# Four graph layers on one core: root products ahead of the upper sums, and column marks made by ScalarE

## The chip, the cores and the metric

The kernel runs on one core of a Trainium2 chip. Its metric is the device time of one execution in microseconds; the time before is 4219.57 us, the median of three runs (4215.5 to 4219.84).

## The reference

A graph of 100000 nodes with 16 features and 50000 edges passes through four layers. Each layer normalises the nodes (`h = relu(layernorm(x))`), makes a message for each edge from the features at one end of it, sums the messages over the edges that share the other end, and adds to x. Cut to what matters:

```python
edge_index = jnp.stack([src, dst])
h = relu(_layernorm(x)); x = x + clip(h + segment_sum(h[src] * ew * w, dst) + slw * h, 0, 1)
h = relu(_layernorm(x)); x = x + segment_sum(sum_k basis[e, k] * (h[dst] @ W[k]), src)
h = relu(_layernorm(x))
# third layer, once from src to dst and once in reverse, 8 outputs each:
#   g = relu(layernorm(h) * ln_g + ln_b)
#   out = segment_sum(einsum(g[src], (edge_attr @ We + be)), dst) + g @ Wr + bias
x = x + concatenate([out_n, out_r])
h = relu(_layernorm(x))
# fourth layer: m = silu(einsum(h[dst], edge_attr, W_msg)) @ W_lin, agg = segment_sum(m, src)
x = x + h + silu(einsum(h, agg, W_upd)) @ W_upd_lin
```

`g @ Wr + bias` are the third layer's root products: a product for every node, whatever its edges.

## The kernel before, in words

The nodes lie as 128 partitions by 784 nodes by 16 features in SBUF (`x`, `h`). The edges are sorted twice in a first part (by dst and by src), one record per edge, into two tables in HBM; blocks of 14 nodes per partition (`BC`) take their edges in tiles of 128 edges. A sorted edge list has 448 tiles, handled 8 at a time, so that each layer has 56 groups, in 14 rounds of 4 (`RING`).

In a group of the edge stage (`edges(l)` and, for PE and POOL, the loops of the same stage):

- SP loads the records of the group (`rec`), as soon as the group four before it has been spread out (`e["spread"]`) and its marks are made (`e["lo"]`).
- POOL gathers the rows of the table of h by eight indirect DMAs (L478), one for each tile.
- PE transposes the rows (L636), ScalarE copies or scales them to `featT` (L847, L850), PE multiplies them with the layer's weights: products 0 and 1 at L608, 2 and 3 at L584 (`late_product`). The products 2 and 3 share PSUM with the sums.
- VectorE (DVE) multiplies the products with the edge's attributes (L1244, L1257, L1272), reduces them to one message an edge (L1249, L1265, L1277) in `raw`, and spreads the message over the 14 columns (nodes) of its block with the column marks `at_hi` (L1197, `spread_out`): a mark is 1 in the column of the edge's node and 0 elsewhere. DVE makes the marks itself, in `columns` (L1192): `is_equal` of the numbers 0 to 13 and the record's field.
- ScalarE makes the partition marks `at_lo`, 128 wide, from eight Abs (L830) and a Relu (L834): relu(1 - |number - node|) is 1 where both are equal.
- PE sums over the edges by a matmul with those marks, tile by tile (L563), one group behind: in the second and third layers four tiles in `upper_sums`, four in `lower_sums`, the lower ones behind the products' use by DVE. Each fp32 matmul shows as two passes in the trace, so four tiles are `x8`.
- DVE adds the sums tile by tile to a running sum (L1219, `run`), also one group behind, and SP writes it to HBM (`scan`). In these two layers `run` starts only when all eight sums are there.

In the third layer root products are put into the gaps. A group does 2, 2, 2 or 1 blocks of 128 columns of nodes (`BLOCKS`): ScalarE copies a part of h to `rootH` (L838), PE transposes it (L615), ScalarE makes `rootT` (L855), PE multiplies it with `Wroot` into `psR` (`root_products`, L625), and DVE adds that and the bias to x at the group's end (`root`, L1301 and L1303). `psR` shares its PSUM bank with `raw`, so DVE's reduction L1265 waits for the root products of its group (`root_s["sums"]`). The root products wait for `rootT` (`rowsS`) and for DVE's add of the group before (`added`).

Each engine works through its instructions in the order in which the program writes them; the waits are semaphores set by hand. Of the code these lines set the order on PE:

```python
for m in range(2, 4):
    late_product(g, m)
if not first:
    upper_sums(g)
if l == 2:
    root_products(i, k, first)
if not first:
    lower_sums(g)
```

In the first and fourth layers PE's group ends with the sums and matmuls without use (`spin`, L543) between them; in the second they stand behind the lower sums; the third has none. Between the edge stages lie node stages (`nodes(l)`), which read the sums from HBM, add them to x, normalise and store the table. `W4` is a weight table for the last part (the update of the fourth layer), made by DVE (L1341) from a product of PE.

## Time and profile before

| | |
|---|---|
| median of three runs | 4219.57 us |
| profiled execution | 4218.45 us |
| its span | 4216.7 us |
| PE, DVE, ScalarE (ACT), POOL busy | 2432.8, 2864.7, 1201.1, 2737.6 us |
| first sorting and its placing by POOL | to about 562 us |
| edges of the first layer | 562 to 1126 us |
| placing of the second table by POOL | 1126 to 1628 us |
| edges of the second layer | 1628 to 2263 us |
| nodes, then edges of the third layer | 2263 to 2409, then to 3097 us |
| nodes, then edges of the fourth layer | 3097 to 3193, then to 3765 us |
| update of the fourth layer | 3765 to 4217 us |

The span runs from the first to the last instruction of the profiled execution. A stage's own limit is read from its own stretch, since busy shares over the whole span mix four kinds of stage. A group's time is the distance between two starts of the same instruction in neighbouring groups. In the rows, `xN` merges N neighbours of one line, and the bracket at the end tells how long the engine stood idle and what released it.

### The profile page before, as it was taken

The page shows a single profiled execution, that of the slowest core. Times are in us where ns is not written, and L with a number is a line of the kernel's source. Part 1 is how long each engine was busy: PE and PEld are TensorE (multiplying, and loading weights), DVE is VectorE, ACT ScalarE, POOL GpSimd, SP SyncE. Part 2 cuts the span into 40 slices and gives each one's busy share as a digit, 9 for nine tenths or more (in the row PEclk, how much of TensorE's full clock was granted, in tenths as well). Part 3 has the DMA queues.
Part 4 walks back from the last instruction along what each step waited for, and adds up shares of the span by engine and source line. Part 5 has one row for each costly group of instructions (what it writes and reads, how often), then busy time and mean ns, then how long its engine had stood idle before and what let it go on. Part 6 is the DMA issues. An engine that isn't in the chain of part 4 may idle for free.

```text
span 4216.7 us, 32712 instructions
## 1 busy us (share of the span) xinstructions
PE 2432.8 (58%) x9418; PEld 1746.0 (41%) x9418; DVE 2864.7 (68%) x4332; ACT 1201.1 (28%) x3002; POOL 2737.6 (65%) x2799
## 2 busy tenths in 40 slices
PE   1200038788600003888883077777725988979998
PEld 1100037777500002656562055555513777753333
DVE  8893035666580003999998877777776887868887
ACT  1000023333430002444443244444413343421111
POOL 3777777777777777776660176666505777746776
PEclk7555579999855556888886577777767999985556
DMA  6011023333630001333344222222532333351010
GB/s 181 9 26 52 8 51 111 103 111 103 104 114 12 5 5 28 99 90 98 94 94 98 83 77 91 91 92 92 82 126 91 102 108 100 109 91 30 26 35 27
DMA packets 200536, 321.45 MB, mean 76 GB/s; under 512 B 83898, under 2 KB 166698, under 8 KB 199971
## 3 DMA queue, kind: packets, MB, share of 16 engines
q1 hardware_dynamic: 112848, 265.61, 17.8%
q0 software_dynamic: 82368, 21.64, 8.1%
q10 hardware_dynamic: 5140, 32.09, 2.0%
q8 instruction: 76, 1.25, 0.1%
q14 instruction: 104, 0.85, 0.1%
HBM read 66.90 MB, written 252.21 MB: 76 GB/s over the span
## 4 chain that ended last, share of the span: by engine, by line
POOL 39%; DVE 24%; issue 19%; PE 14%; ACT 2%; DMA 1%; SPq 1%; POOLq 0%; DVEq 0%
POOL rows L478 21%; POOL edges_by_dst L462 9%; POOL edges_by_src L462 9%; DVE work L1219 8%; PE psX L720 6%; PE psK L563 5%; DVE natD L1244 3%; DVE psX L1249 3%; PE psX L625 2%; DVE natS L1354 1%; DVE psX L1265 1%; DVE h L1105 1%; ACT work L830 1%; PE psK L700 1%; DVE psX L1102 1%
## 5 line engine op out<-in xcount | busy, mean ns | idle before, releaser
L478 POOL DMA_INDIRECT rows<-table,rec x1792 | 1692.2, 944 | 996.5 <-issue 522.8
L563 PE MATMUL psK<-work 128*128 128x224 f32 x3584 | 974.2, 429 | 518.3 <-DVE work L1197 292.5
L563 PEld LDWEIGHTS psK<-work 128*128 128x128 f32 x3584 | 816.0, 236 | 704.4 <-issue 646.8
L1219 DVE SCALAR_TENSOR_TENSOR work<-work,keep,psK 128x224 f32<-128x224 f32 x1792 | 800.9, 447 | 109.6 <-PE psK L563 52.1
L830 ACT ACTIVATE work<-iota,rec 128x128 f32<-128x128 f32 x1792 | 546.0, 391 | 575.4 <-PE psK L563 358.1
L543 PE MATMUL psX<-keep,ident 128*128 128x256 f32 x2648 | 636.3, 388 | 0.0
L543 PEld LDWEIGHTS psX<-keep,ident 128*128 128x128 f32 x2648 | 520.9, 197 | 63.0 <-issue 1.5
L462 POOL DMA_INDIRECT edges_by_dst<-natD,pos x391 | 374.6, 958 | 184.2 <-issue 127.0
L462 POOL DMA_INDIRECT edges_by_src<-natS,pos x391 | 374.4, 958 | 127.3 <-issue 127.3
L1197 DVE TENSOR_TENSOR work<-at_hi,psX 128x1792 f32<-128x1792 f32 x224 | 452.2, 2019 | 6.2 <-ACT psX L872 0.4
L636 PE MATMUL psX<-ident,rows 128*128 128x128 f32 x168 | 49.7, 296 | 657.0 <-DMA rows<-table,rec 657.0
L509 POOL TENSOR_TENSOR work<-natS 128x512 f32<-128x512 f32 x196 | 243.4, 1257 | 156.2 <-DVE natS L1354 156.2
L850 ACT ACTIVATE natD<-psX 128x128 f32<-128x128 f32 x112 | 31.0, 277 | 1049.2 <-PE psX L636 1049.2
L720 PE MATMUL psX<-natD,work 32*128 32x512 f32 x784 | 303.9, 1036 | 18.8 <-DVE natS L1354 18.1
L636 PEld LDWEIGHTS psX<-ident,rows 128*128 128x128 f32 x168 | 23.8, 142 | 682.4 <-issue 497.5
L1228 DVE TENSOR_TENSOR psX<-rows,rec 128x128 f32<-128x128 f32 x56 | 16.9, 301 | 425.3 <-DMA rows<-table,rec 425.3
L1354 DVE TENSOR_TENSOR natS<-psX,h 128x1024 f32<-128x1024 f32 x196 | 238.5, 1217 | 73.1 <-PE psX L720 73.0
L1237 DVE TENSOR_TENSOR natD<-hats 128x128 f32<-128x128 f32 x56 | 15.9, 284 | 382.1 <-ACT hats L821 382.1
L834 ACT ACTIVATE work<-work,one 128x1024 f32<-128x1024 f32 x224 | 257.2, 1148 | 7.3
L584 PE MATMUL psK<-natD 32*128 32x512 f32 (+1 forms) x448 | 210.1, 601 | 67.0 <-DVE work L1219 66.7
L608 PE MATMUL psX<-natD 32*128 32x512 f32 (+2 forms) x672 | 173.6, 594 | 91.3 <-ACT natD L847 50.2
L1265 DVE TENSOR_REDUCE psX<-natD 128x64 f32<-128x576 f32 x112 | 79.5, 756 | 130.8 <-PE psX L625 130.8
(149 smaller groups left out, 2478.4 us busy)
## 6 DMA issues: line engine op xcount, KB each, us to landing
scan<-work SPq DMA_DIRECT2D x224, 896.0 KB
rows<-table,rec POOLq DMA_INDIRECT x1792
table<-h ACTq DMA_DIRECT2D x28, 896.0 KB, 3.6
work<-scan SPq DMA_DIRECT2D x168, 112.0 KB, 2.0
rec<-edges_by_dst SPq DMA_DIRECT2D x112, 84.0 KB, 1.9
natD<-scan SPq DMA_DIRECT2D x56, 112.0 KB, 2.0
edges_by_dst<-natD,pos POOLq DMA_INDIRECT x391
edges_by_src<-natS,pos POOLq DMA_INDIRECT x391
```

The source lines that it names most:

```text
L462: pool.indirect_dma_start(out=rec_by[s].ap(), out_offset=bass.IndirectOffsetOnAxis(ap=pos[s][0:n, u:u + 1], axis=0), in_=nat[0:n, u * F:(u ...
L478: pool.indirect_dma_start(out=rows[k][:, u * D:(u + 1) * D], out_offset=None, in_=table.ap(), in_offset=bass.IndirectOffsetOnAxis(ap=rec[k ...
L509: nc.gpsimd.tensor_tensor(hf, w[:, :, :, 0:8], w[:, :, :, 8:16], ALU.add).then_inc(up["half"], 1)
L543: nc.tensor.matmul(psT[:, 256:512], ident[:, :], keep[0][:, 0:256], start=True, stop=True)
L563: nc.tensor.matmul(psK[:, o:o + BW], at_lo[par][:, t * P:(t + 1) * P], spread[par][:, t * BW:(t + 1) * BW], start=True, stop=True)\
L584: nc.tensor.matmul(psK[:, (m - 2) * 512:(m - 2) * 512 + w.shape[1]], featT[row:row + high, s * P:(s + 1) * P], w[row:row + high, :], start ...
L720: k = nc.tensor.matmul(psQ[q % 2][:, j * 512:(j + 1) * 512], rt[two, b * P:(b + 1) * P], W4[two, m * 512:(m + 1) * 512], start=True, stop= ...
L830: a = S.activation(at_lo[par][:, t * P:(t + 1) * P], iota1[:, :], ACT.Abs, bias=field(l, k, LO[ORDER[l]])[:, t, :])
L834: S.activation(at_lo[par], at_lo[par], ACT.Relu, scale=-1.0, bias=one[:, :]).then_inc(e["lo"], 1)
L1197: V.tensor_tensor(spread[par].rearrange("p (u c f) -> p u c f", c=BC, f=D), v3(at_hi[par][:, :], BC)[:, :, :, None].to_broadcast([P, G, BC ...
L1219: V.scalar_tensor_tensor(acc[par][:, t * BW:(t + 1) * BW], was, keep[s][:, bass.ds(q * G + t, 1)], psK[:, o:o + BW], ALU.mult, ALU.add).th ...
L1354: V.tensor_tensor(products(q)[0], psQ[q % 2].rearrange("p (u k i) -> p u k i", k=D, i=D), v3(h[:, bass.ds(c * CW + 64 * q, 64)])[:, :, Non ...
```

## The change

Three things change.

1. In PE's order of the third layer `root_products` stands ahead of `upper_sums`, behind the late products.
2. The column marks `at_hi` are made by ScalarE (`column_of`: eight Abs of 128x14 and one Relu of 128x112), ahead of the partition marks, in every group of every layer. The wait for the sums of two groups before (`summed`) now stands ahead of both. `columns` is gone from DVE, and L1197 waits for a new semaphore `cols`. The record's field has the other sign, so that Abs can take it as bias.
3. DVE makes `W4` behind the node stage of the third layer, no longer at the end of the second layer's edges.

```diff
                         for m in range(2, 4):
                             late_product(g, m)
+                        if l == 2:
+                            root_products(i, k, first)
                         if not first:
                             upper_sums(g)
-                        if l == 2:
-                            root_products(i, k, first)
                         if not first:
                             lower_sums(g)
...
-                def partition_of(i, k, started):
+                def column_of(i, k):
 
                     par = k % 2
-                    if started:
-                        act.wait_ge(e["summed"], i * (RING * G) + (k - 1) * G)
+                    for t in range(G):
+                        a = S.activation(at_hi[par][:, t * BC:(t + 1) * BC], iota14[:, :], ACT.Abs,
+                                         bias=field(l, k, HI[ORDER[l]])[:, t, :])
+                    a.then_inc(e["colsraw"], 1)
+                    act.wait_ge(e["colsraw"], i * RING + (k + 1))
+                    S.activation(at_hi[par][:, :], at_hi[par][:, :], ACT.Relu, scale=-1.0, bias=one[:, :])\
+                        .then_inc(e["cols"], 1)
+
+                def partition_of(i, k):
...
-                    partition_of(i, k, started)
+                    if started:
+
+                        act.wait_ge(e["summed"], i * (RING * G) + (k - 1) * G)
+                    column_of(i, k)
+                    partition_of(i, k)
...
-                own.did(V.scalar_tensor_tensor(fields[:, :, HI[s]], ki[5][:, 0:NAT], -float(BC), ki[3][:, 0:NAT],
-                                               ALU.mult, ALU.add))
+                own.did(V.scalar_tensor_tensor(fields[:, :, HI[s]], ki[5][:, 0:NAT], float(BC), ki[3][:, 0:NAT],
+                                               ALU.mult, ALU.subtract))
...
-                def columns(i, k):
-
-                    dve.wait_ge(rec_in[k], i * 16 + (PAST_REC[l] + 16))
-                    own.did(V.tensor_tensor(v3(at_hi[k % 2][:, :], BC), iota14[:, None, :].to_broadcast([P, G, BC]),
-                                            field(l, k, HI[s]).to_broadcast([P, G, BC]), ALU.is_equal))
-
-                def spread_out(k):
+                def spread_out(i, k):
                     par = k % 2
+                    dve.wait_ge(e["cols"], i * RING + (k + 1))
...
-                edges(l)
-                if l == 1:
+                if l == 2:
                     dve.wait_ge(w4_psum, 1)
...
                     k.then_inc(w4_ready, 1)
+                edges(l)
```

The third layer on PE, one group with two blocks of nodes, before: the rows that wait name the semaphores (`r_` those of the root products, `e2_` those of the third layer's edges).

```order
L563 MATMUL psK<-work 128x224 [waits e2_run,e2_lo,e2_spread]
L563 MATMUL psK<-work 128x224 x3
L625 MATMUL psX<-natD 128x128 [waits r_added,r_rowsS]
L625 MATMUL psX<-natD 128x128 x3
L563 MATMUL psK<-work 128x224 [waits e2_used]
L563 MATMUL psK<-work 128x224
L563 MATMUL psK<-work 128x224 [waits e2_used]
L563 MATMUL psK<-work 128x224
L615 MATMUL psX<-ident,natD 128x128 [waits r_rows,gath2]
```

And now:

```order
L625 MATMUL psX<-natD 128x128 [waits r_added,r_rowsS]
L625 MATMUL psX<-natD 128x128 x3
L563 MATMUL psK<-work 128x224 [waits e2_run,e2_lo,e2_spread]
L563 MATMUL psK<-work 128x224 x3
L563 MATMUL psK<-work 128x224 [waits e2_used]
L563 MATMUL psK<-work 128x224
L563 MATMUL psK<-work 128x224 [waits e2_used]
L563 MATMUL psK<-work 128x224
L615 MATMUL psX<-ident,natD 128x128 [waits r_rows,gath2]
```

The four matmuls of the root products, which wait for DVE's add of the group before, have come ahead of the four upper sums; the eight sums now lie behind one another, up to the next group's transposes.

The third layer on ScalarE, one group, now (L856 and L864 are the lines L847 and L855 of before, L847 here is L838, L839 and L843 are L830 and L834):

```order
L856 ACTIVATE natD<-psX,shift,gain 128x128 [waits e2_bandT]
L856 ACTIVATE natD<-psX,shift,gain 128x128
L864 ACTIVATE natD<-psX,shift,gain 128x256 x2
L847 ACTIVATE natD<-h 128x256
L828 ACTIVATE at_hi<-iota,rec 128x14 [waits e2_summed,rec1]
L828 ACTIVATE at_hi<-iota,rec 128x14 x7
L832 ACTIVATE at_hi<-at_hi,one 128x112 [waits e2_colsraw]
L839 ACTIVATE work<-iota,rec 128x128 x8
L843 ACTIVATE work<-work,one 128x1024 [waits e2_abs]
```

The three rows of `at_hi` are new and stand between the copy of h and the partition marks; all else is in its old order.

## Rows read from the trace of the kernel before

**Rows 1.** Busy time in four stretches, the edges of the four layers; the columns are named.
```profile
core 0: us, PE busy (x) PEld busy (x) DVE busy (x) ACT busy (x) POOL busy (x), PEclk, DMA share, GB/s
562.00:1126.00 564.00, 442.15 (x1944) 391.69 (x1944) 333.66 (x644) 201.15 (x505) 423.74 (x449) 0.92 0.38 101
1628.00:2263.00 635.00, 541.37 (x1849) 376.77 (x1850) 594.86 (x889) 275.47 (x840) 422.76 (x448) 0.81 0.33 90
2409.00:3097.00 688.00, 489.26 (x1890) 377.67 (x1890) 519.32 (x1007) 302.80 (x783) 423.40 (x448) 0.78 0.32 86
3193.00:3765.00 572.00, 497.15 (x2219) 395.76 (x2219) 443.35 (x707) 223.24 (x606) 422.70 (x448) 0.96 0.37 98
```

**Rows 2.** Waits of DVE in the third layer: in total, times, longest.
```profile
DVE psX L1265 <- PE psX L625: 125.2, 53, 3.1
```

**Rows 3.** Timeline of one third-layer group: start us, us, engine, line, instruction.
```profile
2624.58 3.33 PE L563 MATMUL psK<-work 128*128 128x224 f32 x8 [1.28 <-DVE work L1219]
...
2627.70 1.10 PE L625 MATMUL psX<-natD 128*128 128x128 f32 x8
...
2628.64 1.68 PE L563 MATMUL psK<-work 128*128 128x224 f32 x8
...
2628.91 1.42 DVE L1265 TENSOR_REDUCE psX<-natD 128x64 f32<-128x576 f32 x2 [2.04 <-PE psX L625]
...
2630.36 2.02 DVE L1197 TENSOR_TENSOR work<-at_hi,psX 128x1792 f32<-128x1792 f32 x1
...
2632.30 3.82 DVE L1219 SCALAR_TENSOR_TENSOR work<-work,keep,psK 128x224 f32<-128x224 f32 x8
...
2632.48 2.44 ACT L830 ACTIVATE work<-iota,rec 128x128 f32<-128x128 f32 x8
...
2636.04 0.41 DVE L1301 TENSOR_TENSOR x<-x,psX 128x256 f32<-128x256 f32 x1
```

**Rows 4.** The same timeline, PE: starts of the sums, root products and transposes.
```profile
2600.98 3.19 PE L563 MATMUL psK<-work 128*128 128x224 f32 x8 [1.28 <-DVE work L1219]
...
2612.08 3.33 PE L563 MATMUL psK<-work 128*128 128x224 f32 x8 [1.27 <-ACT work L834]
...
2618.74 0.38 PE L615 MATMUL psX<-ident,natD 128*128 128x128 f32 x2
...
2630.16 0.38 PE L615 MATMUL psX<-ident,natD 128*128 128x128 f32 x2
...
2636.27 3.33 PE L563 MATMUL psK<-work 128*128 128x224 f32 x8 [1.03 <-DVE work L1219]
...
2639.39 1.91 PE L625 MATMUL psX<-natD 128*128 128x128 f32 x8
...
2642.79 0.27 PE L615 MATMUL psX<-ident,natD 128*128 128x128 f32 x1
...
2648.77 1.46 PE L563 MATMUL psK<-work 128*128 128x224 f32 x3 [1.27 <-DVE work L1219]
```

**Rows 5.** Timeline of a second-layer group, DVE and ScalarE.
```profile
1804.89 0.91 ACT L817 ACTIVATE hats<-rec,hatb 128x16 f32<-128x16 f32 x4
...
1806.09 2.43 ACT L830 ACTIVATE work<-iota,rec 128x128 f32<-128x128 f32 x8
...
1808.69 0.28 DVE L1237 TENSOR_TENSOR natD<-hats 128x128 f32<-128x128 f32 x1
...
1808.90 0.27 DVE L1192 TENSOR_TENSOR at_hi<-iota,rec 128x112 f32<-128x112 f32 x1
...
1809.19 1.29 DVE L1244 TENSOR_TENSOR natD<-psX,natD 128x512 f32<-128x512 f32 x2
...
1814.04 2.02 DVE L1197 TENSOR_TENSOR work<-at_hi,psX 128x1792 f32<-128x1792 f32 x1
```

**Rows 6.** The same stretch, POOL: one of eight gathers of a group.
```profile
1809.27 0.94 POOL L478 DMA_INDIRECT rows<-table,rec  x1 [0.30 <-issue]
```

**Rows 7.** Timeline, DVE: the table W4, and the first product of layer three.
```profile
2266.54 3.91 DVE L1341 TENSOR_SCALAR natD<-psX,rowmask 128x256 f32<-128x256 f32 x8
...
2423.68 0.82 DVE L1257 TENSOR_TENSOR natD<-psX,rec 128x288 f32<-128x288 f32 x2 [17.95 <-PE psX L608]
```

More of the change, by code:

```diff
@@ L238, in build_gnn @@
         names = ("taken", "bandT", "bandS", "prod", "used", "preact", "silu", "hats", "hatsraw",
-                 "abs", "lo", "spread", "summed", "run")
+                 "abs", "lo", "colsraw", "cols", "spread", "summed", "run")
         lacks = [("bandT", "bandS", "prod", "used", "preact", "silu", "hats", "hatsraw"),
@@ L822, in hat_factors @@
                         .then_inc(e["hats"], 1)
-                def partition_of(i, k, started):
+                def column_of(i, k):
                     par = k % 2
-                    if started:
-                        act.wait_ge(e["summed"], i * (RING * G) + (k - 1) * G)
+                    for t in range(G):
[6 more added lines that the diff above has]
+                def partition_of(i, k):
+                    par = k % 2
                     for t in range(G):
@@ L1183, in nodes_twice @@
                 own.close()
-            STEPS = [2, 3, 3, 1]
+            STEPS = [1, 2, 2, 0]
             def edges(l):
                 s, e = ORDER[l], ed[l]
-                def columns(i, k):
-                    dve.wait_ge(rec_in[k], i * 16 + (PAST_REC[l] + 16))
-                    own.did(V.tensor_tensor(v3(at_hi[k % 2][:, :], BC), iota14[:, None, :].to_broadcast([P, G, BC]),
-                                            field(l, k, HI[s]).to_broadcast([P, G, BC]), ALU.is_equal))
-                def spread_out(k):
+                def spread_out(i, k):
                     par = k % 2
+                    dve.wait_ge(e["cols"], i * RING + (k + 1))
                     V.tensor_tensor(spread[par].rearrange("p (u c f) -> p u c f", c=BC, f=D),
@@ L1229, in messages @@
                                         field(l, k, D_EW).to_broadcast([P, G, D]), ALU.mult).then_inc(e["taken"], 1)
-                        columns(i, k)
                         dve.wait_ge(e["taken"], g + 1)
@@ L1239, in messages @@
                                                 hv[:, :, 1, None, :].to_broadcast([P, G, 4, 4]), ALU.mult))
-                        columns(i, k)
                         own.settle()
@@ L1251, in messages @@
                     elif l == 2:
-                        columns(i, k)
                         for m in range(4):
@@ L1268, in messages @@
                     else:
-                        columns(i, k)
                         for m in range(2):
@@ L1288, in group @@
                     own.settle()
-                    spread_out(k)
+                    spread_out(i, k)
                     if l != 3 and not first:
```

## The prediction

> **What bounds the kernel now.** I read the busy times by stage first [rows 1]. In the first layer's edges POOL, with its eight gathers a group, sets the pace: 564 us over 56 groups are 10.1 us a group, and eight gathers of 0.94 us with 0.30 us between them are about 10.0 [rows 6]. The fourth layer is alike (572 us with filling and draining). The second layer is another case: VectorE (DVE) is busy 594.86 of 635 us, a group takes about 11.0 us, more than POOL needs. The third layer, 688 us, is the slowest: neither DVE (519) nor POOL (423) nor PE (489) fills it, so the engines wait for one another. What that wait is, the waits of DVE say: 53 times, 125.2 us in all, its reduction L1265 stands until PE's root products L625 are done, 2.36 us a time [rows 2]. The timeline of one group shows why [rows 3]: PE first does the four upper sums (L563, 3.12 us until the next instruction), which nobody wants yet, and only then the root products, for which DVE stands 2.04 us. The upper sums come in a stretch of low clock: eight passes take 3.33 us there, 1.68 us in the lower half. Four groups take 47.79 us, 11.95 each [rows 4]. That is the number to beat.
>
> **Part 1, the order on PE in the third layer.** Nothing is added, four or eight passes of L625 move ahead of eight passes of L563. Two limits remain for DVE.
>
> First, its own work. From group to group 11.69 us went by (PE 2624.58 to 2636.27), of which DVE waited 2.04: 9.65 us of work, and 0.19 us less without the columns (part 2), 9.46.
>
> Second, a wait that takes the place of the old one. DVE's running sums L1219 want all eight sums of the group, and these now stand behind the root products; the root products in turn want DVE's add L1301 of the group before (semaphore r_added), which is behind its running sums. So the loop is: running sums 3.74 us until the add (2632.30 to 2636.04), add 0.41, release of PE 0.15 (2636.12 to 2636.27), PE's block of 24 passes, release of DVE 0.1 (an estimate, from the 0.15 of PE). Today the block, from the first upper sum to the next transposes L615, takes 6.66, 5.58 and 6.52 us [rows 3, 4], 6.25 on average, with eight root passes. With four root passes (every fourth group) it is shorter by half of L625's time, between 0.47 and 0.95, say 0.7: 5.55. The loop is 4.40 plus the block: 10.65 and 9.95, on average 10.5 us, if PE's clock stays as it is. It was granted 0.78 of full speed in this stage and 0.81 in the second layer, where PE is busy 541 of 635 us; the third layer now keeps PE busy 489 of 688, 8.7 us a group, and at about 10.3 us a group that share is the second layer's 0.85. So I take 0.81 and a block shorter by 4%: 6.02 and 5.35, groups of 10.42 and 9.75, on average **10.25 us**. Bounds: above, 10.5 with the clock of today; below, POOL's 10.0. Saving (11.95 - 10.25) x 54 groups = **92 us**; bounds 78 and 105. I count 54 of 56, since the first group has no sums and the last none after it.
>
> **Part 2, the columns.** DVE loses 224 instructions of 0.27 us (L1192). In the second layer, where DVE is the bound, L1244 starts 0.29 us after L1192; without it, it starts when L1237 is done, at 1808.97 plus the usual 0.03, so 0.19 us earlier [rows 5]: 56 x 0.19 = **10.6 us**. In the third layer this lies inside the loop's wait in most groups; in the first and fourth POOL sets the time: nothing.
> ScalarE gets nine instructions for each. The nearest row: four Abs of 16 columns and one Relu of 64 take 1.20 us (1804.89 to 1806.09), 0.20 per Abs and 0.40 for the Relu, so eight and one are 2.05 us. The upper bound is the pace of the 128-column Abs, 2.43 us for eight, plus 0.4: 2.8. Who waits? The new wait is DVE's: the spreading L1197 now waits for `cols` too. In the second layer the columns would be ready at 1808.14 and the spreading starts at 1814.04: 5.9 us of room. In the third, ScalarE is ready for them 0.2 us after DVE's running sums start (2632.48 against 2632.30); but in the new order PE's block ends, and the transposes start, only 0.1 us ahead of those, not 2.14, so ScalarE comes 2.2 us after. The next spreading is 9.46 - 1.94 = 7.5 us after the start of the running sums (1.94 is 2630.36 to 2632.30), so the room is 7.5 - 2.2 - 2.05 = 3.2 us. Behind the columns stand ScalarE's own Abs of the marks `at_lo`, wanted by PE one group later, and the Silu of the fourth layer, which DVE wants only after a whole turn of running sums. The load fits: in the first layer ScalarE is busy 3.6 us a group, in the third 5.4, plus 2.05. SP's refill of `rec` waits for `lo` as well, and `lo` still comes before the spreading ends or close to it, three groups ahead of its use. Term: 0.
>
> **Part 3, the table W4.** Eight instructions, 3.91 us together (L1341), go from the end of the second layer to behind the third layer's node stage. There they run while DVE waits 17.95 us for the first gather [rows 7]; where they were, DVE waited for a load anyway. PE is held until they are done, but has nothing to do earlier. Term: 0; if that cover were gone, 3.9 us.
>
> **Sum.** 92 + 10.6 = 102.6 us off the profiled execution's 4218.45, 4115.9; the median of the runs is 1.1 higher: **4117 us**.
>
> **Rivals.**
> A, PE at full clock through the third layer. The block is then about 4.3 us (0.94 us for the root products as between 2627.70 and 2628.64, and 1.68 twice), the loop 8.7, and POOL's 10.0 is the bound: (11.95 - 10.0) x 54 = 105, in all 4219.6 - 115.9 = 4104 us. For it: the clock was 0.92 and 0.96 in the layers that keep PE busy with filler. Against: the second layer is as full as this will be and has 0.81. The Trainium skill, "TensorE: Matmul & The Clock Gate", Part 1, says that the throttled clock is the default and activity releases it; by that rule alone a denser PE gives this time. The first and fourth layers agree with it, the second only in part.
> B, the block stays as long as today or gets longer, because root products and upper sums now both fall in the slow stretch: 10.5 to 10.9 us a group, 78 to 57 us saved there, 4131 to 4152 us.
> C, ScalarE's columns come late, and all of it ends slower. It decides from 3.2 us of room: nine instructions above 5.3 us make DVE wait, above 7.3 us the gain is gone. At 8 us (0.9 each) the third layer's group is 10.25 + 2.7 = 12.95, 54 us more than today, less 10.6: 4263 us. Against: a 16-column activation takes 0.31 us at most in [rows 5], a third of that. The Trainium skill, "ScalarE: Activation LUTs", Rules for kernel authors, sends relu, max, add and mul to VectorE; by it one DVE instruction of 0.27 us becomes 2.05 us of ScalarE for nothing. On this trace that holds for work and not for time, as DVE is the engine waited for.
> D, PE at low clock throughout the third layer: a block of 3.12 + 1.7 + 3.12 = 7.9 us, 12.3 and 11.5 a group, 12.1 on average: 8 us lost, 10.6 won, 4217 us, no change.
>
> **Chances.** Forecast 0.67, A 0.13, B 0.15, C 0.02, D 0.03. About 0.2% (8 us) is what a measurement of this kernel can tell from no change. The forecast, A and B are faster: 0.95; D is the same, 0.03; C slower, 0.02. The range takes in A and the better half of B, since both bounds of the block lie in it: 4098 to 4142 us.
>
> **What would show it.** Third layer: about 10.25 us from group to group, stage near 595 us, L1265's wait on L625 under 0.3 us, a new wait of DVE L1219 for PE L563 of about 0.8 us on average, uneven from group to group, clock near 0.81. Second layer: 10.8 us a group, DVE still without a gap. First and fourth: same length. ScalarE about 2 us a group busier, no wait of L1197's successor for it. Wrong if the third layer's group is above 10.6 or exactly POOL's 10.0, or if DVE waits for ScalarE's Relu.

## The result and the profile after

The changed kernel takes **4111.34 us**, median of four runs (4110.35 to 4116.54), against 4219.36 for the kernel before beside it. The ratio is 0.9748, 95% interval 0.9732 to 0.9765: 108 us or 2.5% faster, 6 us below the forecast of 4117 and inside its range. The profiled span is 4108.9 us, before it was 4216.7.

Where the time went is told by the length of each layer's edges, from its first gather's start to the end of its last running sum:

| layer | before | after | difference | forecast |
|---|---|---|---|---|
| first | 581.3 | 580.3 | -1.0 | 0 |
| second | 636.0 | 626.0 | -10.0 | -10.6 |
| third | 687.5 | 592.1 | -95.4 | -92 |
| fourth | 590.5 | 585.1 | -5.4 | 0 |

These differences come to 111.9 us, the span's to 107.8; the first sorting, the placing of the second table and the update of the fourth layer are 1.0, 1.1 and 1.8 us longer in the trace after. From the end of the second layer's edges to the third's first gather there are 142.8 us before and 142.7 after, so the table W4 costs nothing in its new place.

The page after: the engines, and the chain of work that ended last. Line numbers of VectorE (DVE) are shifted: running sums L1219 is L1227 now, the spreading L1197 is L1205, the reduction L1265 is L1270, the product L1257 is L1262, the add L1301 is L1305.

```profile
PE 2346.3 (57%) x9418; PEld 1697.5 (41%) x9418; DVE 2832.2 (69%) x4108; ACT 1634.5 (40%) x5018; POOL 2738.8 (67%) x2799
...
POOL 45%; DVE 21%; issue 20%; PE 11%; DMA 2%; SPq 1%; ACT 0%; POOLq 0%; DVEq 0%
```

POOL is in 45% of the chain (39% before) and PE in 11% (14%). ScalarE's 1634.5 us are 433 more than the 1201.1 before, for 2016 more instructions. That is 1.93 us for each of 224 groups; the forecast said about 2.

Busy time in the edges of the second and third layers after, the view of [rows 1]: length, busy time (and instructions) of PE, its weight loads, DVE, ScalarE and POOL, granted clock, DMA share, GB/s.

```profile
1628.00:2250.00 622.00, 528.93 (x1832) 371.24 (x1832) 582.52 (x828) 385.40 (x1344) 423.57 (x449) 0.81 0.34 91
2395.00:2995.00 600.00, 413.29 (x1890) 332.86 (x1890) 518.25 (x961) 413.12 (x1288) 423.75 (x448) 0.82 0.39 101
```

The third layer's PE is busy 413 us for the same 1890 matmuls as in [rows 1], where it was 489, with a granted clock of 0.82 instead of 0.78. DVE is busy 518 us of 600, before it was 519 of 688: what is gone is waiting.

The waits of the third layer after (2450 to 2980 us), against [rows 2] (2450 to 3080 us): in total, times, longest.

```profile
PE psX L615 <- DMA rows<-table,rec: 55.0, 31, 4.9
...
PE psX L625 <- DVE x L1305: 45.0, 34, 1.6
DVE work L1227 <- PE psK L563: 16.6, 16, 1.5
DVE psX L1270 <- PE psX L625: 13.7, 20, 1.3
```

The 125.2 us for which DVE stood at the reduction are 13.7; over the whole layer 130.8 us are 16.2. The wait that takes its place, the running sums for the upper sums, is 16.6 us in 16 groups. PE now waits, for DVE's add (45.0 us) and for the gathered rows (55.0 us).

POOL's gathers of the third layer, before and then after: shortest, median and longest in ns, then the start of the first and of the last.

```profile
L478 POOL DMA_INDIRECT rows<-table,rec x448: 938/944/1185, 2409.4 to 3051.4; - x150
```
```profile
L478 POOL DMA_INDIRECT rows<-table,rec x448: 940/944/1192, 2400.5 to 2959.6; - x150
```

Before, they were spread over 642.0 us, and POOL stood 95.6 us in 42 waits for the records (`rec`), which SP loads only when an earlier group has been spread out. After, they take 559.1 us, 10.0 us a group from the first to the last, as in the first and fourth layers (558.8 and 558.0 us); the waits for records are gone. Of the layer's 95.4 us, 82.9 lie in this stretch and the rest behind the last gather (45.4 us before, 33.1 after).

Two groups of the third layer after, the view of [rows 3, 4], first with a low clock in PE's block and then without:

```profile
2869.03 2.04 PE L625 MATMUL psX<-natD 128*128 128x128 f32 x8 [1.60 <-DVE x L1305]
...
2870.87 5.26 PE L563 MATMUL psK<-work 128*128 128x224 f32 x16
...
2871.18 1.42 DVE L1270 TENSOR_REDUCE psX<-natD 128x64 f32<-128x576 f32 x2 [0.38 <-PE psX L625]
...
2875.96 0.38 PE L615 MATMUL psX<-ident,natD 128*128 128x128 f32 x2
...
2876.16 3.83 DVE L1227 SCALAR_TENSOR_TENSOR work<-work,keep,psK 128x224 f32<-128x224 f32 x8 [1.51 <-PE psK L563]
...
2878.29 1.68 ACT L828 ACTIVATE at_hi<-iota,rec 128x14 f32<-128x14 f32 x8
...
2880.00 0.39 ACT L832 ACTIVATE at_hi<-at_hi,one 128x112 f32<-128x112 f32 x1
...
2880.30 2.43 ACT L839 ACTIVATE work<-iota,rec 128x128 f32<-128x128 f32 x8
...
2880.47 1.13 PE L625 MATMUL psX<-natD 128*128 128x128 f32 x8 [1.60 <-DVE x L1305]
...
2881.44 3.19 PE L563 MATMUL psK<-work 128*128 128x224 f32 x16
...
2883.73 2.02 DVE L1205 TENSOR_TENSOR work<-at_hi,psX 128x1792 f32<-128x1792 f32 x1
...
2884.47 0.27 PE L615 MATMUL psX<-ident,natD 128*128 128x128 f32 x1
...
2885.67 3.82 DVE L1227 SCALAR_TENSOR_TENSOR work<-work,keep,psK 128x224 f32<-128x224 f32 x8
```

In the first, root products and sums take from 2869.03 to the transposes at 2875.96, 6.93 us, and DVE's running sums stand 1.51 us. In the second the same 24 passes take 4.00 us (2880.47 to 2884.47), and DVE has no wait. ScalarE's columns take from 2878.29 to 2880.30, where its next work starts: 2.01 us. The spreading that needs them starts at 2883.73, 3.3 us after the Relu's end. POOL's gathers come every 1.25 us.

The same two blocks in the view of [rows 1]; the clock granted to PE is the figure after the last bracket, 0.57 and 1.00 of full speed.

```profile
2869.03:2875.96 6.93, 6.93 (x24) 6.49 (x25) 5.21 (x8) 2.64 (x7) 5.10 (x7) 0.57 0.45 146
2880.47:2884.47 4.00, 4.00 (x25) 3.95 (x26) 3.93 (x8) 3.40 (x9) 2.99 (x4) 1.00 0.66 236
```

### The profile page after: what moved, and what is told of

The parts are those of the page before. It is cut to its first block, busy times and chain, and to the rows that moved or that the text cites. A ratio compares the mean times of both kernels' runs of the same rounds, so it can differ in the third digit from the quotient of the medians.

```text
span 4108.9 us, 34672 instructions
## 1 busy us (share of the span) xinstructions
PE 2346.3 (57%) x9418; PEld 1697.5 (41%) x9418; DVE 2832.2 (69%) x4108; ACT 1634.5 (40%) x5018; POOL 2738.8 (67%) x2799
## 3 DMA queue, kind: packets, MB, share of 16 engines
q8 instruction: 76, 1.25, 0.1%
## 4 chain that ended last, share of the span: by engine, by line
POOL 45%; DVE 21%; issue 20%; PE 11%; DMA 2%; SPq 1%; ACT 0%; POOLq 0%; DVEq 0%
POOL rows L478 27%; POOL edges_by_dst L462 9%; POOL edges_by_src L462 9%; DVE work L1227 7%; PE psX L720 6%; DVE natD L1250 3%; DVE psX L1255 3%; PE psK L563 2%; DVE natS L1358 1%; DMA rows<-table,rec 1%; PE psK L700 1%; DVE h L1118 1%; DVE psX L1115 1%; PE psK L691 1%; PE psX L625 0%
## 5 line engine op out<-in xcount | busy, mean ns | idle before, releaser
L563 PE MATMUL psK<-work 128*128 128x224 f32 x3584 | 904.6, 409 | 450.0 <-DVE work L1205 292.4
L563 PEld LDWEIGHTS psK<-work 128*128 128x128 f32 x3584 | 783.6, 225 | 602.6 <-issue 552.5
L1227 DVE SCALAR_TENSOR_TENSOR work<-work,keep,psK 128x224 f32<-128x224 f32 x1792 | 801.2, 447 | 120.7 <-PE psK L563 62.4
L828 ACT ACTIVATE at_hi<-iota,rec 128x14 f32<-128x14 f32 x1792 | 375.2, 296 | 463.2 <-PE psK L563 245.7
L839 ACT ACTIVATE work<-iota,rec 128x128 f32<-128x128 f32 x1792 | 544.3, 386 | 0.0
L1205 DVE TENSOR_TENSOR work<-at_hi,psX 128x1792 f32<-128x1792 f32 x224 | 452.3, 2019 | 8.2 <-ACT psX L885 2.4
L1244 DVE TENSOR_TENSOR natD<-hats 128x128 f32<-128x128 f32 x56 | 15.9, 285 | 383.0 <-ACT hats L821 383.0
L843 ACT ACTIVATE work<-work,one 128x1024 f32<-128x1024 f32 x224 | 257.3, 1149 | 7.2
L753 ACT ACTIVATE work<-h 128x1792 f32<-128x1792 f32 x28 | 47.5, 1697 | 374.7 <-DVE h L1118 374.7
```

The costliest lines, as they stand in the source:

```text
L563: nc.tensor.matmul(psK[:, o:o + BW], at_lo[par][:, t * P:(t + 1) * P], spread[par][:, t * BW:(t + 1) * BW], start=True, stop=True)\
L828: a = S.activation(at_hi[par][:, t * BC:(t + 1) * BC], iota14[:, :], ACT.Abs, bias=field(l, k, HI[ORDER[l]])[:, t, :])
L839: a = S.activation(at_lo[par][:, t * P:(t + 1) * P], iota1[:, :], ACT.Abs, bias=field(l, k, LO[ORDER[l]])[:, t, :])
L843: S.activation(at_lo[par], at_lo[par], ACT.Relu, scale=-1.0, bias=one[:, :]).then_inc(e["lo"], 1)
L1205: V.tensor_tensor(spread[par].rearrange("p (u c f) -> p u c f", c=BC, f=D), v3(at_hi[par][:, :], BC)[:, :, :, None].to_broadcast([P, G, BC ...
L1227: V.scalar_tensor_tensor(acc[par][:, t * BW:(t + 1) * BW], was, keep[s][:, bass.ds(q * G + t, 1)], psK[:, o:o + BW], ALU.mult, ALU.add).th ...
```

## The experiments

The runs fall in two sets. In one, four kernels run on chip 5, the kernel before took 4216.3 us, close to the 4219.36 above. In the other, eight kernels on the chips 9, 4 and 14, it took 5059 to 5079 us itself, and the profile differs in kind. They are told apart, the first set first; ratios are against the kernel before in the same set.

**e5_cols3: more work for ScalarE.** Does the room that part 2 of the prediction gives ScalarE exist, and how large is it?

```diff
+for t in range(2 * G):
+    S.activation(scrap[:, t * BC:(t + 1) * BC], iota14[:, :], ACT.Abs,
+                 bias=field(l, k, HI[ORDER[l]])[:, t % G, :])
 (ahead of the eight Abs of the columns, in every group)
```

> The changed kernel with 24 Abs for the columns in every group, sixteen of them into a scratch tile: 3.3 us more work of ScalarE a group. My theory: the third layer's ScalarE then has 7.4 + 3.3 = 10.7 us of work a group and becomes the bound, and the columns use up the room of 3.2 us: group 10.7 to 11.0 us, 25 to 45 us more than the changed kernel; second layer 0 (7.1 + 3.3 of 10.8 us, room 5.9). Rival: columns so early that all is hidden, 0; or all of it on the path, 3.3 us a group, 180 us.

4140.34 us, ratio 0.9817 (0.9802 to 0.9832), 29 us above the changed kernel. The layers take 580.2, 628.5, 619.1 and 588.3 us. The third layer of e5_cols3 from 2642 on, and DVE's wait of that layer:

```profile
2643.02 3.25 ACT L829 ACTIVATE scrap<-iota,rec 128x14 f32<-128x14 f32 x16
...
2647.88 0.39 ACT L836 ACTIVATE at_hi<-at_hi,one 128x112 f32<-128x112 f32 x1
...
2648.37 2.02 DVE L1209 TENSOR_TENSOR work<-at_hi,psX 128x1792 f32<-128x1792 f32 x1 [0.58 <-ACT at_hi L836]
...
2653.47 3.25 ACT L829 ACTIVATE scrap<-iota,rec 128x14 f32<-128x14 f32 x16
```
```profile
DVE work L1209 <- ACT at_hi L836: 40.4, 48, 2.5
```

The expectation held: the group takes 10.67 us and the kernel 29 us more. ScalarE's turn is 10.45 us (2643.02 to 2653.47) with no gap, and the spreading waits for its Relu 48 times, 0.84 us each. So an added 3.25 us more than uses up the room in the third layer. In the second layer, where the prediction gave 5.9 us, nothing is seen: its 628.5 us are those of e6_spin too, which has no extra Abs. Nor in the first. Rival C's mechanism exists, and the change stays below it. The prediction let it begin at 5.3 us of columns; here they take 5.25 (2643.02 to 2648.27) and DVE waits already, as ScalarE's whole turn has become the group. Where between 2.01 and 5.25 us the wait begins, no run of this set shows.

**e6_spin: fillers ahead of the root products.** Rival A said that a PE at full clock would leave POOL's gathers as the bound, at 10.0 us a group and 4104 us.

```diff
     late_product(...)
 if l == 2:
+    pe.wait_ge(root_s["rowsS"], g + 1)
+    spin(2)
+if l == 2:
     root_products(i, k, first)
```

> The changed kernel with two filler matmuls (four passes) between the late products and the root products of the third layer, where PE waits 1.6 us for DVE's add. They keep PE's clock up. My theory (blocks of 7.1 us at low clock are what is left above POOL's pace, blocks at full clock take 4.16): third layer's group 10.21 to 10.0, granted clock above 0.9, 8 to 14 us less than the changed kernel, 4098 to 4104. Rival (the fillers delay the root products, and the pace is POOL's anyway): 0 or a few us more.

4106.6 us (4101.69 to 4110.08), ratio 0.9737 (0.9724 to 0.975). The interval overlaps the changed kernel's, so the 5 us between the medians are not told from nothing. Expected were 8 to 14 us and a clock above 0.9, and neither came. The third layer takes 588.6 us, 10.11 us a group against 10.21, with 2114 matmuls:

```profile
2403.00:2992.00 589.00, 434.77 (x2114) 340.75 (x2114) 510.67 (x954) 412.93 (x1287) 424.18 (x448) 0.89 0.37 100
```
```profile
DVE psX L1273 <- PE psX L625: 28.4, 21, 2.6
```
```profile
PE psX L615 <- DMA rows<-table,rec: 67.2, 43, 4.6
```

The clock is 0.89; the changed kernel has 0.83 in the same stretch. The running sums have no wait left but one at the layer's end (the reduction has 28.4 us in 21 groups), and in four neighbouring groups the sixteen sums took 3.19 us each. Yet the gathers take 559.5 us from first to last, for 559.1 in the changed kernel; only the time behind the last of them is shorter, 29.2 for 33.1 us. A quicker PE had nothing more to give, as POOL was not being held back.

**e8_seven: the same with seven gathers of eight.** Is POOL the bound that is reached?

```diff
+GATHERS = [8, 8, 7, 8]
-for u in range(G):
+for u in range(GATHERS[l]):
 (the waits for the gathers count 16 * GATHERS[l])
```

> The kernel with fillers and seven gathers a group in the third layer (the eighth tile of each group keeps an older group's rows, so the third layer's messages of one tile in eight are left wrong). Theory (with PE at full clock, POOL's eight gathers at 10.0 us a group are the bound): group down to DVE's own 9.46 us, 25 to 30 us less than the kernel with fillers. Rival (DVE or PE is the bound already): 0, apart from the 1.25 us of a first group's gathering.

The kernel leaves out one gather of eight in the third layer, so that one tile in eight takes the rows of an older group.

4074.17 us, ratio 0.966 (0.9645 to 0.9675): 32.4 us below e6_spin, somewhat more than the 25 to 30 expected. The third layer takes 556.0 us, a group 9.54, and past its start PE no longer waits for gathered rows:

```profile
2403.00:2960.00 557.00, 451.85 (x2114) 343.77 (x2114) 509.33 (x952) 412.97 (x1287) 370.41 (x392) 0.92 0.36 106
```
```profile
DVE psX L1274 <- PE psX L626: 5.7, 9, 1.3
```

DVE stands there 5.7 us in 480 us of the layer, and POOL now waits for records (41.6 us), so 9.54 is DVE's own work; the prediction had 9.46 for it. The gathers thus hold e6_spin back by 0.57 us a group. In the changed kernel both limits are near: the gathers at 10.0 us, unheld from first to last, and the loop over PE and DVE at about 10.26.

**e7_old_order_spin: columns on ScalarE, order as before, fillers.** It was to raise PE's clock without the new order, and so to part the two.

```diff
     late_product(...)
+if l == 2:
+    pe.wait_ge(root_s["rowsS"], g + 1)
+    spin(2)
 if not first:
     upper_sums(g)
+if l == 2:
+    root_products(i, k, first)
 (against the changed kernel; W4 stands at its old place too)
```

> The columns alone (old order on PE) with the same two filler matmuls ahead of the upper sums. It asks whether the order or the clock was worth the gain. At full clock the upper sums take 1.5 us and the root products 0.94, so the root products would be ready 0.5 to 1.0 us after DVE asks for them, not 2.4. My theory: group 10.2 to 10.9 us, 55 to 95 us less than the kernel before, that is, the low clock was most of the price of the old order. Rival (the order itself is the price): group over 11.4 us, under 35 us less.

4203.59 us, ratio 0.997 (0.9958 to 0.9982). The layers take 581.2, 626.1, 690.0 and 584.4 us. Third layer of e7_old_order_spin: its window, DVE's wait, and one group of the timeline.

```profile
2401.00:3091.00 690.00, 553.30 (x2114) 419.31 (x2114) 509.10 (x952) 412.87 (x1287) 423.56 (x448) 0.78 0.31 86
```
```profile
DVE psX L1273 <- PE psX L625: 122.1, 47, 3.8
```
```profile
2605.66 2.07 PE L543 MATMUL psX<-keep,ident 128*128 128x256 f32 x4
2607.53 3.19 PE L563 MATMUL psK<-work 128*128 128x224 f32 x8
...
2611.68 1.68 PE L563 MATMUL psK<-work 128*128 128x224 f32 x8
...
2611.95 1.42 DVE L1273 TENSOR_REDUCE psX<-natD 128x64 f32<-128x576 f32 x2 [3.68 <-PE psX L625]
```

The clock did not rise, 0.78 as before: the two filler matmuls (four passes) fell in the slow stretch themselves and took 2.07 us, where in 31 of 56 groups of e6_spin they took 1.13. So this kernel doesn't part clock and order, and its expectation (55 to 95 us less) was missed. It does something else: it is the columns and fillers without the order. The second layer has its 10 us less (626.1), the fourth its 6 less (584.4), and the third is no shorter (690.0 against 687.5), with a wait of 122.1 us at the reduction.

Against e6_spin it differs in nothing but PE's order and the place of W4, which costs nothing (142.7 us between the stages in both). So the order, with columns and fillers on both sides, is worth 101.4 us in the third layer (690.0 against 588.6) and 97.0 us of the kernel (4203.59 against 4106.6).

**The other set.** Here the same kernel before takes 5059 to 5079 us; no trace of it is kept. The nearest is e3_w4, which is the kernel before but for the place of W4 (5084.43 us, below). The kernel before of the first set and then e3_w4, a row each on DVE's running sums and on PE's filler matmuls: count, busy time, mean ns, then the idle time ahead of them and what ended it.

```profile
L1219 DVE SCALAR_TENSOR_TENSOR work<-work,keep,psK 128x224 f32<-128x224 f32 x1792 | 800.9, 447 | 109.6 <-PE psK L563 52.1
...
L543 PE MATMUL psX<-keep,ident 128*128 128x256 f32 x2648 | 636.3, 388 | 0.0
```
```profile
L1219 DVE SCALAR_TENSOR_TENSOR work<-work,keep,psK 128x224 f32<-128x224 f32 x1792 | 801.7, 447 | 1138.0 <-remote 893.2
...
L543 PE MATMUL psX<-keep,ident 128*128 128x256 f32 x2648 | 729.1, 412 | 264.7 <-issue 261.3
```

A running sum takes 447 ns in both. But ahead of them stand 1138.0 us of idle time for 109.6, of which 893.2 were ended by something that the trace only calls remote (it ran on one core), and ahead of PE's fillers 261.3 us ended by nothing that the profile shows ("issue"), where there was none. The first layer, 581 us before, takes 1126 us in e3_w4 and 1310 in e11_order_again. PE in the first layer of e11_order_again:

```profile
1205.82 0.77 PE L543 MATMUL psX<-keep,ident 128*128 128x256 f32 x1 [0.85 <-issue]
1207.92 0.59 PE L543 MATMUL psX<-keep,ident 128*128 128x256 f32 x1 [1.33 <-issue]
```

Fillers wait for no engine, and they start one at a time with 0.85 to 1.33 us between them. PE is late with its own instructions; what makes it so, these runs do not show. What a placement on PE costs here says little of the kernel in the first set.

e1_order and e11_order_again are the kernel before with the new order alone.

```diff
+if l == 2:
+    root_products(i, k, first)
 if not first:
     upper_sums(g)
-if l == 2:
-    root_products(i, k, first)
```

> The kernel before with the root products ahead of the upper sums in the third layer, nothing else. My theory (the order gives nine tenths of the gain): third layer's group from 11.93 to about 10.3 us, second layer unchanged at 11.0, 88 to 95 us less than before, 4125 to 4132 us. Rival (order and columns need each other, since DVE would still be held by its own column instruction): under 60 us less.

> The kernel before with the root products ahead of the upper sums in the third layer, nothing else; once more, since the first time the kernel before itself took 5072 us there. My theory (the order gives nine tenths of the gain): third layer's group from 11.93 to about 10.3 us, second and fourth layers unchanged at 636 and 590 us, 88 to 95 us less than before. Rival (order and columns need each other): under 60 us less.

5160.53 us, ratio 1.0202 (1.0152 to 1.0251), and 5174.55 us, ratio 1.0193 (1.0156 to 1.0231): about 2% slower, twice, where 88 to 95 us less were expected. Third layer 824.2 and 829.8 us, against 742.0 in e3_w4. Their groups in that layer take 9.7 to 9.9 us and 18.6 to 19.8 us in turn, almost throughout. e2_columns and e12_columns_again are the changed kernel with the old order and W4 at its old place (the diff above turned round).

> The changed kernel with the old order on PE and W4 at its old place: the columns on ScalarE alone. My theory: second layer's group 11.0 to 10.82 us, 10 us less; in the third layer DVE reaches its wait for the root products 0.19 us earlier and waits 0.19 us longer, 0; first and fourth 0: 4209 us. Rival (the fourth layer's end, 5.4 us shorter in the changed kernel, comes from the columns): 15 us less, with the fourth layer's stretch near 585 us in place of 590.

> The changed kernel with the old order on PE and W4 at its old place: the columns on ScalarE alone; once more, since the first time the kernel before itself took 5072 us there. My theory: second layer 10 us shorter (636 to 626), third 0, 4206 to 4209 us. Rival (the fourth layer's end, 590.5 us before and 585.1 after the change, comes from the columns too): 15 us less in all, with 585 us in the fourth layer; if it is chance, it differs between runs of one kernel.

5096.77 us, 1.0083 (1.005 to 1.0116), and 5034.8 us, 0.9963 (0.9936 to 0.999): the same kernel on both sides of 1, so differences of about 1% mean nothing here. Their second layers take 769.1 and 738.9 us (782.8 in e3_w4), too far apart to tell the 10 us that were expected of the columns. Their third layers take 756.0 and 749.3 us, some 75 less than with the order alone. So in this condition the order costs 68 to 88 us in the layer in which it gains 101 in the first set. DVE's waits in the third layer, e11_order_again and then e12_columns_again:

```profile
DVE natD L1257 <- remote: 163.0, 51, 9.5
...
DVE natD L1257 <- issue: 41.6, 13, 4.5
```
```profile
DVE psX L1270 <- PE psX L625: 65.0, 25, 3.5
...
DVE psX L1270 <- remote: 43.6, 8, 7.3
DVE psX L1270 <- issue: 41.0, 18, 3.7
```

In the new order DVE waits at its products L1257 (204.6 us), in the old at the reduction (149.6 us). A group of e11_order_again:

```profile
3298.47 0.76 PE L608 MATMUL psX<-natD 64*128 64x288 f32 x4 [1.74 <-issue]
...
3299.06 0.65 PE L584 MATMUL psK<-natD 64*128 64x288 f32 x4
...
3302.59 2.36 PE L563 MATMUL psK<-work 128*128 128x224 f32 x8
...
3306.08 0.46 DVE L1257 TENSOR_TENSOR natD<-psX,rec 128x288 f32<-128x288 f32 x1 [3.80 <-issue]
...
3310.98 0.46 DVE L1257 TENSOR_TENSOR natD<-psK,rec 128x288 f32<-128x288 f32 x1 [4.44 <-remote]
...
3311.49 3.35 PE L563 MATMUL psK<-work 128*128 128x224 f32 x8 [6.54 <-DVE natD L1257]
```

PE has done all four products by 3299.71. DVE's second and third multiplication of them come with holes of 3.80 and 4.44 us all the same, and the lower sums, 6.54 us idle, start only when DVE has done the third. So the results were there, and DVE is late as PE is above. Why, and why the new order draws these holes into every second group, these runs do not show.

e3_w4 is the kernel before with the table W4 moved alone.

```diff
+if l == 2:
+    (the eight instructions of W4)
 edges(l)
-if l == 1:
-    (the eight instructions of W4)
```

> The kernel before with W4 made behind the third layer's node stage, nothing else. My theory: 0, under 1 us either way, because DVE waits for a load at the old place and for the first gather at the new one. Rival: 3.9 us more or less, the eight instructions' time, if one of the two covers is not there.

5084.43 us, ratio 1.0022 (0.9992 to 1.0051): no difference to be seen within that 1%. e4_cols2 is e5_cols3 with eight extra Abs in place of sixteen.

> The changed kernel with sixteen Abs for the columns in every group, eight of them into a scratch tile: 1.6 us more work of ScalarE a group. My theory (3.2 us of room in the third layer, 5.9 in the second): 0, within 3 us of the changed kernel, 4108 to 4116 us. Rival C (the columns are already close to late): half of the added 1.6 us shows in each third-layer group, 45 us more.

5254.06 us, 1.0364 (1.031 to 1.0418), layers of 1211.1, 790.7, 856.8 and 827.7 us. The changed kernel itself was not timed in this set, so the extra Abs can't be priced; e5_cols3 was made for that. e9_old_order_full_clock is e2_columns with fillers at three places of the third layer, and e10_fill is the changed kernel with fillers at three.

```diff
 (e9)  spin(2) ahead of the late products, spin(2) behind them, spin(2) behind lower_sums
 (e10) spin(2), as above; spin(1) behind the late products; spin(2) behind lower_sums
```

> The columns alone (old order on PE) with two filler matmuls at three places of the third layer's group: between the products 1 and 2, behind product 3, behind the lower sums. In the earlier run the fillers fell into the low stretch and kept nothing up (0.78, as before); these fill the two gaps of 1.0 and 1.3 us around the late products. Clock theory (the low stretch is most of the price of the old order): clock over 0.9, root products ready under 0.6 us after DVE asks, group 10.0 to 10.3 us, third layer 583 to 600 us, total 4100 to 4120. Order theory (the upper sums ahead are the price by themselves): third layer over 650 us, total over 4165.

> The changed kernel (new order) with fillers in the third layer: two between the products 1 and 2, one behind product 3, two behind the lower sums. Theory (what is left above POOL's pace in the changed kernel is the blocks of 7.1 us at low clock): clock over 0.95, no block over 5 us, group 10.0, third layer 580 to 586 us against 592, total 6 to 12 us under the changed kernel, 4099 to 4106. Rival (POOL's last gathers and their landing set the end anyway): within 3 us of the changed kernel.

5191.7 us, 1.0224 (1.0185 to 1.0264), third layer 846.6; and 5210.38 us, 1.029 (1.0241 to 1.0339), third layer 894.9. Both are inconclusive on what the clock is worth: in this condition the layer of e9_old_order_full_clock is 91 to 97 us longer than that of e2_columns and e12_columns_again, which have no fillers, and that of e10_fill 65 to 71 us longer than with the order alone.

## Why the prediction was right

**The old wait and the new one.** The step "what is behind the wait on L625" held: the reduction's wait fell from 125.2 to 13.7 us, under 0.3 us a group as forecast, and a wait of the running sums for L563 came, 0.3 us a group where 0.8 was forecast.

**The length of the block.** Here a term was mis-sized. The prediction took one block of 6.02 us (5.35 with four root passes) for all groups, from a clock between 0.78 and 0.81. The block with four root passes was too long already for the kernel before, 5.55 us in the prediction and 4.98 (2600.98 to 2605.97) in the trace. After, from the first root product to the end of the last sum, the 54 blocks take 5.20 us on average, against 6.10 before. There is no one block. From 2737 to 2941 us the groups of a round take 4.16, 7.10, 4.16 and 6.44 us in turn (the last with four root passes), where they took 6.82, 5.73, 6.68 and 5.14 before: PE is at full clock through a whole block or at low clock through most of one. The 4.16 is rival A's block (4.3), the 7.10 comes close to rival D's (7.9). Ahead of that stretch the blocks lie between 4.16 and 6.50 us without such a pattern. A block of 7.10 puts the loop at 11.4 us (2869.03 to 2880.47), one of 4.16 lets DVE run at its own pace, about 9.5. With these lengths the prediction's loop is right: 21 groups from 2729 to 2945 us take 10.26 us each, against the forecast 10.25.

**What bounds the layer.** This step was wrong for most of the layer, and luck hid it. The prediction let the loop over PE and DVE set the pace and POOL's 10.0 us be only the lower bound; a group of exactly 10.0 was to be a sign of being wrong. Over the layer's first 30 groups the spreadings are 10.01 us apart, and PE waits for gathered rows in 29 of them (46.4 us, 2425 to 2726): there the gathers set the pace, as in rival A, with the clock at 0.85 and not at full speed. Then 21 groups go at the loop's 10.26 us, but POOL gathers ahead and is not held back by it: PE's transposes start 2.4 us behind the start of their group's last gather at first and 7.6 us behind it in the end. The last two spreadings are 13.1 and 13.3 us apart, because PE stands 4.9 and 4.5 us for the last groups' rows, until 10.4 and 14.5 us behind the start of their last gather; why these land so late, no run shows. So the layer begins and ends with PE waiting for rows, and what the loop had fallen behind in between (21 times 0.25 us) was caught up before the end. Averaged over all, a group takes 10.21 us; without the last two it is 10.09. e6_spin and e8_seven say the same: with a quicker PE the kernel is no clear step faster, with fewer gathers it is 32 us faster. The forecast of 10.25 lies near the mean of three stretches with different limits.

**The third layer's saving.** 95.4 us for 92. It is the order's: with columns and fillers on both sides, the order is worth 101.4 us in this layer (e7_old_order_spin against e6_spin). That includes what the order does to the clock, 0.89 against 0.78; how much of the old order's price was the low clock, no run parts. The order without columns was measured only in the other set, where it came out slower; that it gives as much by itself in the first set, no run shows.

**The second layer.** 10.0 us for 10.6. The step was that DVE loses the start of L1192; after, the masks' product L1250 starts 0.32 us behind L1244, where L1244 started 0.50 us behind L1237 [rows 5]:

```profile
2002.52 0.28 DVE L1244 TENSOR_TENSOR natD<-hats 128x128 f32<-128x128 f32 x1
...
2002.84 1.29 DVE L1250 TENSOR_TENSOR natD<-psX,natD 128x512 f32<-128x512 f32 x2
```

0.18 us times 56 is 10.1 us. e7_old_order_spin has the same stage length, 626.1, without the other two parts.

**ScalarE's room.** Columns 2.01 us for 2.05; room 3.3 for 3.2; no wait of the spreading for the Relu in the third layer; with 3.25 us more the wait is there. This is rival C tried, at one size. The Trainium skill, "ScalarE: Activation LUTs", Rules for kernel authors, sends relu, max, add and mul to VectorE and so would have kept the columns there; by busy time it is right (0.27 against 2.01 us), and in the layer that VectorE bounds the exchange still gives 10 us.

**W4.** Forecast 0, measured 142.8 against 142.7 us between the stages, and 142.7 in e7_old_order_spin, with W4 at its old place. e3_w4, in the other set, shows no difference either.

**What was missed.** The fourth layer is 5.4 us shorter, forecast 0. It is 585.1 here and 584.7, 584.4 and 584.7 in e6_spin, e7_old_order_spin and e8_seven, against 590.5 in the one trace of before; 588.3 with the extra Abs. The difference lies behind the last gather (32.5 us before, 27.0 after; the gathers take 558.0 us in both), in the last five groups, whose spreadings are 12.3, 13.6, 10.7, 13.5 and 13.3 us apart before and 12.4, 11.1, 16.2, 9.3 and 9.2 after, while the gathers keep 9.99 us in both. Either DVE's 0.27 us a group tell there, or it is how the last landings fall in that one trace. No run parts the two; it is open.

**Rival A** had the right bound, POOL's gathers, and the wrong way there: it wanted PE at full clock throughout, and the gathers went at their pace with 0.82. Its 105 us also lacked the late landing of the last rows, 14.5 us behind the start of the last gather, for 2.4 at first. e6_spin tried more clock, and got some 5 us at most. **Rival B** (a longer block) is true of every second group between 2737 and 2941 us and not of the mean. **Rival D** fell with the clock of 0.82.

## What to carry to other kernels

Look at what an engine does between the start of a wait and its end: here PE did 3 us of sums that nobody wanted yet ahead of products that an engine stood waiting for, and exchanging them was worth 95 to 101 us without removing an instruction. Follow the loop that remains, with each release in it, and compare it with the pace of every other engine. Where two limits lie as near as 10.25 and 10.0 us, forecast both: a loop that is slower in some groups only, with buffers between, need not hold the faster engine back. Look for it in that engine's own trace, here the first and the last gather. Work may go to an engine that needs seven times as long for it, when the room until the result is wanted is known from the timeline, and can be tried by adding work till the wait appears.

## What the runs showed of the hardware

- **PE's clock in a repeating pattern.** The same 24 passes take 4.0 or 6.9 us in neighbouring groups of the changed kernel, at a granted clock of 1.00 (2.4 GHz) and 0.57 (mostly 1.2 GHz), from 2737 to 2941 us. The full clock is not a property of a stage here, and the stage's mean (0.82) belongs to no group of that stretch.
- **Fillers do not make a clock.** Two filler matmuls a group ahead of the slow stretch left 0.78 at 0.78 (e7_old_order_spin) and ran slow themselves, 2.07 for 1.13 us. In the new order the same two took the clock from 0.83 to 0.89 (e6_spin).
- **The same kernel 20% longer.** 5059 to 5079 us for 4216 on other chips. In e3_w4 the running sums (447 ns), ScalarE's Abs (391 ns) and the gathers (944 ns) take what they took before, PE's matmuls somewhat more (fillers 412 for 388 ns, sums 448 for 429), and PE and DVE stand idle ahead of instructions whose inputs are there. In that condition the order costs 68 to 88 us in the third layer, where it gains 101 in the other. A comparison of two orders holds for the condition in which it is made.
- **Gathers that set a pace.** 448 gathers take 558.0 to 559.5 us wherever nothing holds them back (first, third and fourth layers of the changed kernel, and the third of e6_spin), 1.25 us each. Where PE waits for their rows, it goes on 2.4 us behind the start of a group's last gather, but in the last two groups of the third layer 10.4 and 14.5 us behind it.
